# One pipeline for a ternary feed-forward network, with part of its preparation taken in the attention before it

## The reference, cut to what matters

```python
def _layernorm(x):            # what stands ahead of every sublayer
    return (x - mean(x)) / sqrt(var(x) + 1e-5)
def rmsnorm(x, weight):
    return x * rsqrt(mean(x * x) + 1e-5) * weight
def activation_quant(x):      # per row (token)
    scale = 127.0 / clip(max(abs(x)), 1e-05)
    return clip(round(x * scale), -128, 127) / scale
def weight_quant(w):          # one scale for the whole matrix; values -1, 0, 1
    scale = 1.0 / clip(mean(abs(w)), 1e-05)
    return clip(round(w * scale), -1, 1) / scale
def bitlinear(x, w):
    return einsum('bsh,oh->bso', activation_quant(x), weight_quant(w))
x_norm = rmsnorm(x, norm_weight)                     # 256 wide
gate, up = split(bitlinear(x_norm, w_gate_up))       # w_gate_up: 1408 x 256
hidden = square(relu(gate)) * up                     # 704 wide
return bitlinear(hidden, w_down)                     # w_down: 256 x 704
```

## Time and profile before

| What | Value |
|---|---|
| Median of 3 runs | 3785.6 us (3783.56 to 3797.69) |
| Profiled execution | 3776.57 us, span 3774.7 us |
| PE busy | 2875.6 us (76% of the span) |
| DVE busy | 2273.3 us (60%) |
| ACT busy | 1493.7 us (40%) |
| POOL busy | 885.2 us (23%) |

### The profile page before, as it was taken

One profiled execution on the slowest core, in us unless ns is written; L12 is line 12 of the kernel. 1 busy time (PEld: TensorE's weight loads), 2 busy tenths in 40 slices (PEclk: granted clock), 3 DMA queues, 4 the chain that ended last, 5 costly groups with the idle time before them and its releaser, 6 DMA issues. The chain is left out here.

```text
span 3774.7 us, 60424 instructions
## 1 busy us (share of the span) xinstructions
PE 2875.6 (76%) x19922; PEld 1822.1 (48%) x19922; DVE 2273.3 (60%) x5171; ACT 1493.7 (40%) x3091; POOL 885.2 (23%) x1241
## 2 busy tenths in 40 slices
PE   5388885465899993399716599899979839999993
PEld 4233334222555552233303377444547638888782
DVE  7699983676677775633467788788869730000003
ACT  5277771254222225399614355222235302121110
POOL 3111110376233336211100033000023261111110
PEclk7599995798999995599857799999989859999996
DMA  8766633499222224478100153000034321111204
GB/s 262 176 118 118 121 90 134 159 367 359 88 82 80 80 75 170 114 134 118 26 24 0 45 168 104 2 1 1 1 96 141 102 83 55 46 59 48 84 27 134
DMA packets 261309, 386.20 MB, mean 102 GB/s; under 512 B 56321, under 2 KB 188654, under 8 KB 260768
## 3 DMA queue, kind: packets, MB, share of 16 engines
q1 hardware_dynamic: 234192, 312.76, 31.1%
q0 software_dynamic: 25152, 68.22, 5.2%
q10 hardware_dynamic: 1680, 1.57, 0.2%
HBM read 227.75 MB, written 160.24 MB: 103 GB/s over the span
## 5 line engine op out<-in xcount | busy, mean ns | idle before, releaser
L3022 POOL DMA_INDIRECT rows_out<-e_out,e_tr_dest x224 | 234.7, 1048 | 872.0 <-DVE e_out L3652 521.2
L1188 ACT ACTIVATE a_pt<-a_psS 128x512 f32<-128x512 f32 x512 | 277.5, 595 | 152.1 <-PE a_psS L1086 147.7
L3652 DVE COPY e_out<-e_psD 128x512 f32<-128x512 f32 x40 | 27.7, 692 | 491.8 <-PE e_psD L3620 491.7
L1210 DVE TENSOR_REDUCE a_mx_sb<-a_psM 128x4 f32<-128x1024 f32 x256 | 292.9, 1215 | 17.2 <-PE a_psM L1069 16.0
L3420 PE MATMUL e_psG<-e_wgu,e_yT 128*128 x576 | 275.1, 600 | 27.0 <-ACT e_yT L3448 24.4
L1100 PE MATMUL a_psV<-a_pt,a_vt 128*18 128x256 f32 x4096 | 291.4, 386 | 1.3 <-issue 0.8
L3620 PE MATMUL e_psD<-e_w,e_hT 128*128 128x256 f32 x1280 | 289.7, 386 | 0.0
L3609 PE MATMUL e_psH<-e_yT,e_w 128*128 128x256 f32 x1280 | 284.4, 381 | 1.6 <-issue 0.8
L3552 ACT ACTIVATE e_hT<-e_psH 128x512 f32<-128x512 f32 x160 | 95.5, 597 | 451.8 <-PE e_psH L3609 451.8
L3620 PEld LDWEIGHTS e_psD<-e_w,e_hT 128*128 128x128 f32 x1280 | 245.8, 195 | 32.8
L3609 PEld LDWEIGHTS e_psH<-e_yT,e_w 128*128 128x128 f32 x1280 | 244.5, 191 | 35.0 <-issue 2.1
(11 more groups left out here) (420 smaller groups left out, 5997.7 us busy)
## 6 DMA issues: line engine op xcount, KB each, us to landing
kbd<-e_bgu SPq DMA_DIRECT2D x64, 512.0 KB, 4.5
cr_kbd<-kbd SPq DMA_DIRECT2D x64, 512.0 KB, 3.4
rows_in<-zeros POOLq DMA_DIRECT2D x36, 522.0 KB, 6.5
e_xin<-rows_in SPq DMA_DIRECT2D x144, 128.0 KB
vbd<-e_bd SPq DMA_DIRECT2D x64, 272.0 KB, 4.2
cr_vbd<-vbd SPq DMA_DIRECT2D x64, 272.0 KB, 2.7
cq_rows<-rows_out SPq DMA_DIRECT2D x32, 512.0 KB, 5.8
e_w<-in_L_ffn_w_dram SPq DMA_DIRECT2D x16, 1024.0 KB, 7.6
```

The lines of the kernel that those rows point to most:

```text
L1188: act.activation(pt[:, probs(t, h), b, :, :], psS[:, unit(t, h, b) % S_BANKS, :].rearrange("p (k c) -> p k c", k=KC), ACT.Exp, scale=scale ...
L1210: dve.tensor_reduce(mx[:, t % 2, :, h, :], psM[:, k % 2, :, :].rearrange("p b (f c) -> p b f c", f=2), AX_X, ALU.max).then_inc(ring_read, 1)
L3022: pool.indirect_dma_start(out=self.rows_out[0:limit, :], out_offset=bass.IndirectOffsetOnAxis(ap=self.dest[:, t:t + 1], axis=0), in_=rows, ...
```

## The change

Two things are done.

First, `phase_norms`, `phase_bit_weights`, `phase_bit_inputs` and `phase_bit_ffn` are replaced for layer 1. A new object, `BitPrelude`, puts their loads, the row statistics, the roots and the sums over the weights into the second attention: SP issues three loads at its tile 20, DVE takes the statistics of tile t - 6 behind its division of tile t and the sums of the two weight matrices at tiles 26 and 28, and POOL computes the two roots of four tiles at a time at every fourth tile, the last two groups behind the loop.

Second, all that is left is one block, `phase_bit`, whose steps are written out without hardware loops. POOL now centres and weights the inputs (two instructions per tile), cuts the down weights, and scales and rounds the 704 hidden values of each tile (two instructions). DVE keeps the row maxima and the quantisation of the inputs, spread over four steps for a group of four tiles, the product with up, the row maximum, the small operations and the residual. The residual of tile s - 3, the product of tile s and part of the inputs of a later group stand in one step of DVE; PE runs gate and up for tile s + 1, the transposes for s - 1 and the down projection for s - 2 in one step. ACT copies the turned weights, in batches of up to four blocks.

```diff
 # phase_attend, POOL
                     if t >= 4:
                         add_tile(t - 4)
+                    if prelude is not None and t >= 11 and t % 4 == 3:
+                        prelude.root(pool, (t - 11) // 4)
                 for t in range(TILES - 4, TILES):
                     add_tile(t)
+                if prelude is not None:
+                    prelude.root(pool, 6)
+                    prelude.root(pool, 7)
 # phase_attend, SP
+                    if t == 20 and prelude is not None:
+                        prelude.load(sp)
 # phase_attend, DVE
                         divide(t, psN[:, 0, :], psN[:, 1, :], scaled)
+                        if prelude is not None and t >= prelude.LAG:
+                            dve.wait_ge(added, t - prelude.LAG + 1)
+                            prelude.survey(dve, t - prelude.LAG)
+                        if prelude is not None and t in (26, 28):
+                            prelude.sum_weights(dve, (t - 26) // 2)
+                    if prelude is not None:
+                        for t in range(TILES - prelude.LAG, TILES):
+                            dve.wait_ge(added, t + 1)
+                            prelude.survey(dve, t)
+class BitPrelude:
...
+    def survey(self, dve, t):
...
+        dve.bn_stats(self.stats[:, t % 2, :], self.core.xs[:, t, :]).then_inc(self.surveyed, 1)
+        dve.wait_ge(self.surveyed, t + 1)
+        dve.bn_aggr(self.core.mv[:, t, :], self.stats[:, t % 2, :]).then_inc(self.averaged, 1)
+    def sum_weights(self, dve, m):
...
+        dve.tensor_reduce(self.part[:, m:m + 1], w[:, :, :].rearrange("p o i -> p (o i)"), AX_X, ALU.add, apply_absolute_value=True).then_inc(self.summed, 1)
+    def root(self, pool, g):
...
+        pool.wait_ge(self.averaged, (g + 1) * self.G)
...      # a Chain of 7 instructions on 4 columns, two of them ALU.pow
+def phase_bit(core, prelude, gate):
...
+                def centre(g, j):
+                    t = g * G + j
+                    if g >= 2:
+                        pool.wait_ge(rounded, g - 1)
+                    pool.tensor_scalar(z[:, g % 2, j, :], core.xs[:, t, :], core.mv[:, t, 0:1], col(prelude.rr, t), ALU.subtract, ALU.mult).then_inc(centred, 1)
+                    pool.wait_ge(centred, t + 1)
+                    pool.tensor_tensor(z[:, g % 2, j, :], z[:, g % 2, j, :], prelude.wb[:, :], ALU.mult).then_inc(z_ready, 1)
...
+                for s in range(FIRST, TILES):
+                    if s == FIRST + G:
+                        cut_down()
+                    g, j = group_at(s, 10)
+                    if g is not None:
+                        centre(g, j)
+                    t = s
+                    if ok(t):
...
+                        pool.wait_ge(scaled, t + 1)
+                        pool.tensor_scalar(flat, flat, col(scale, t), ROUND_MAGIC, ALU.mult, ALU.add).then_inc(h_scaled, 1)
+                        pool.wait_ge(h_scaled, t + 1)
+                        if t >= 2:
+                            pool.wait_ge(q_turned, t - 1)
+                        pool.tensor_scalar(q[:, t % 2, :], flat, ROUND_MAGIC, None, ALU.subtract).then_inc(quantised, 1)
...      # PE
+                for s in range(-2, TILES + 2):
...
+                    if g is not None and j == 0:
+                        turn_inputs(g)
+                    if ok(s + 1):
+                        gate_up(s + 1)
...
+                    if ok(s - 1):
+                        turn_rows(s - 1)
+                    if ok(s - 2):
+                        down(s - 2)
...      # DVE
+                for s in range(-6, TILES + 3):
+                    if ok(s - 3):
+                        residual(s - 3)
+                    t = s
+                    if ok(t):
...
+                        dve.tensor_tensor(flat, psG[:, 2:4, 0:HALF], flat, ALU.mult).then_inc(u_read, 1)
...
+                        dve.tensor_reduce(col(hm, t), flat.rearrange("p a c -> p (a c)"), AX_X, ALU.max, apply_absolute_value=True).then_inc(maxed, 1)
+                    g, piece = group_at(s, 6)
+                    if g is not None and piece != 2:
+                        inputs(g, piece)   # 0: row maxima; 1: six small ones; 3: round 1024 values
+                    if ok(t):
...
+                        c.link(dve.tensor_scalar(col(sm, t), col(hm, t), col(sgd, t), 1e-5 / 127.0, ALU.mult, ALU.max))
+                        c.link(dve.reciprocal(col(rs, t), col(sm, t)))
...
+                        dve.tensor_scalar(col(scale, t), col(rs, t), col(sg3, t), None, ALU.mult).then_inc(scaled, 1)
+                        dve.tensor_scalar(col(out, t), col(sm, t), mu[:, 1:2], gate, ALU.mult, ALU.mult).then_inc(out_ready, 1)
+                    if g is not None and piece == 2:
+                        inputs(g, piece)   # four scalings of 256 values
```

More of the change, by code:

```diff
@@ L1860, in _ @@
             @block.scalar
             def _(act):
[L1862 to L1887, removed]
+                def copy_weights(i):
+                    kind, lo, hi = W_BATCHES[i]
+                    src = bank_of[i % 2][:, 0:(hi - lo) * KC * P].rearrange("p (o k c) -> p o k c", k=KC, c=P)
+                    act.wait_ge(w_turned, i + 1)
+                    if kind == "gu":
+                        for k in range(KC):
+                            ins = act.activation(guT[:, k, lo * P:hi * P].rearrange("p (o c) -> p o c", c=P), src[:, :, k, :], ACT.Copy)
+                        ins.then_inc(w_copied, 1)
+                        return
+                    whole = min(hi, F1 // P)
+                    act.activation(downT[:, lo:whole, :].rearrange("p o (k c) -> p o k c", c=P), src[:, 0:whole - lo, :, :], ACT.Copy).then_inc(w_copied, 1)
+                    if whole < hi:
+                        rows = F1 - whole * P
+                        act.activation(downT[0:rows, whole, :].rearrange("p (k c) -> p k c", c=P), src[0:rows, whole - lo, :, :], ACT.Copy).then_inc(w_copied, 1)
@@ new lines, in _ @@
+                for s in range(-2, TILES + 1):
+                    if s == -2:
+                        for i in range(3):
+                            copy_weights(i)
+                    g, j = group_at(s, 2)
+                    if g is not None and j == 0:
+                        copy_inputs(g)
+                    if ok(s + 1):
+                        relu(s + 1)
+                        square(s + 1)
+                    if s == -1:
+                        for i in range(3, len(W_BATCHES)):
+                            copy_weights(i)
+                    if ok(s - 1):
+                        copy_rows(s - 1)
@@ L1889, in _ @@
             @block.vector
             def _(dve):
+                c = Chain(dve, mu_step)
                 dve.wait_ge(total, 1)
[L1892 to L1899, removed]
@@ new lines, in _, with inputs @@
+                dve.tensor_scalar(tg[:, :, :], w[:, :, :], -1.0, None, ALU.max).then_inc(gu_cut, 1)
+                def inputs(g, piece):
+                    v, rows = g % 2, slice(g * G, (g + 1) * G)
+                    per = 7
+                    if piece == 0:
+                        dve.wait_ge(z_ready, (g + 1) * G)
+                        dve.tensor_reduce(am[:, v, :], z[:, v, :, :], AX_X, ALU.max, apply_absolute_value=True).then_inc(am_step, 1)
+                        dve.wait_ge(am_step, g * per + 1)
+                    if piece == 1:
+                        c = Chain(dve, am_step, g, per, base=1)
+                        c.link(dve.tensor_scalar(am[:, v, :], am[:, v, :], 1e-5, 1.0 / 127.0, ALU.max, ALU.mult))
+                        c.link(dve.reciprocal(s1[:, v, :], am[:, v, :]))
+                        c.link(dve.tensor_scalar(sg[:, v, :], am[:, v, :], mu[:, 0:1], None, ALU.mult))
+                        c.link(dve.tensor_tensor(sg3[:, rows], sg[:, v, :], sg[:, v, :], ALU.mult))
+                        c.link(dve.tensor_tensor(sg3[:, rows], sg3[:, rows], sg[:, v, :], ALU.mult))
+                        c.link(dve.tensor_scalar(sgd[:, rows], sg3[:, rows], 1.0 / 127.0, None, ALU.mult))
+                    if piece == 2:
+                        for j in range(G):
+                            dve.tensor_scalar(za[:, v, j, :], z[:, v, j, :], s1[:, v, j:j + 1], ROUND_MAGIC, ALU.mult, ALU.add).then_inc(z_scaled, 1)
+                    if piece == 3:
+                        dve.wait_ge(z_scaled, (g + 1) * G)
+                        if g >= 2:
+                            dve.wait_ge(i_turned, g - 1)
+                        dve.tensor_scalar(q8[:, v, :, :], za[:, v, :, :], ROUND_MAGIC, None, ALU.subtract).then_inc(rounded, 1)
```

409 lines of the change are left out of this document (201 added, 208 removed).

## The result

The changed kernel takes 3704.2 us, the median of 3 runs (3704.15 to 3704.81), where the kernel before takes 3785.6: a ratio of 0.9784 with a 95% interval of 0.9768 to 0.9799. In a later comparison on one chip it was 0.9793 (0.9775 to 0.9810). The forecast was 3698 us, in a range from 3677 to 3728.

The account below looks back on a forecast made before the run. DVE was taken to bound a tile. 31 + 26 x 4.85 + 5 x 4.2 + 3 + 7.7 = 188.8 us replace 277.7; less 1 in the attention, 88 us off the median 3785.6 gives 3698 us, range 3677 to 3728.

Parts of the forecast that it names:

- The attention, its end, and the prelude: Second attention: the added prelude costs 1 us (bounds 0 and 8); the network's block begins 9.5 us after its end.
- rival D: Second attention: POOL's roots delay its layout of values and PE waits, 24 us, total 3722 us; chance 0.07.
- POOL's rate: POOL's wide one-input instructions run at its copy's rate: 0.42 us for 256 values, 0.81 for 704, 1.43 for 1408.
- Up to the first product: Block start to first product: 17.4 us without collisions, 22 with them, so 31 us behind the attention's end.
- the collision: Before the first product: DVE's cuts and input pieces are held by POOL's instructions, adding 4.5 us.
- A tile: Loop: DVE sets the pace, 4.85 us a tile with inputs (bounds 4.4 and 5.6).
- the prediction's own sign of that: Loop: PE waiting for the rounded hidden values at each tile while DVE idles would show that POOL bounds.
- Rival A: Loop: POOL's wide instructions near 1.6 us, or PE mostly at the lower clock; 5.6 us a tile, 3729 us; chance 0.20.
- Being held: Loop: DVE waits for POOL's instructions, mainly at the input scalings, adding 0.44 us a tile.
- The last tiles and PE: Last five tiles, without inputs: 4.2 us each, between 3.9 and 4.5, at a granted clock of 0.84.
- the ring: Loop: PE's work between two products plus DVE's residual, product and hand-overs; 3.9 us at the upper clock, 5.8 at the lower.
- Drain: From the last product to the end of the last residual: 7.7 us.

Follow-up runs that it names:

- late_prelude: The changed kernel with the prelude's loads, statistics, weight sums and roots in a block of their own behind the attention; 0.9843 of the kernel before.
- both_forms: The changed kernel with POOL's rounding of hidden values and its centring of inputs both written as multiply-adds; 0.9724 of the kernel before.
- balanced: The changed kernel with POOL's rounding and centring as multiply-adds, down weights cut on DVE, inputs scaled and rounded on POOL; 3688.3 us, 0.9710 of the kernel before.
- q_form: The changed kernel with only POOL's rounding of the hidden values written as a multiply-add; 0.9759 of the kernel before.

## Why the prediction was right, and where it was not

The time fell inside the range and 6 us from the forecast. The direction and most of the size rest on the part that held: 20 us of statistics, 30 of weights and 66 of inputs, in which PE hardly worked, now lie beside other work. By the steps of the prediction:

- *The attention, its end, and the prelude.* Right in what the prelude costs. The block starts 9.2 us behind the last addition (9.5 predicted), and rival D did not come (late_prelude). The sign that the attention ends within 1 us of 1868.5 failed: it ended at 1873.6. Of these 5.1 us 2.3 were there at its first copy, before any of the prelude, and 2.8 came within the copies, where late_prelude, without the prelude in its attention, has 3.5.
- *POOL's rate.* The step that failed: "I take the copy's, since it has one input too." Of the forms that this block uses, the copy's rate holds for multiply-add alone. The rounding cost 1.97 us instead of 0.81, the centring 1.22 instead of 0.42, the three cuts 10.2 instead of 4.3. The upper bound of 1.96 ns a value was too low as well: the rounding needs 2.5, and subtract-multiply more. The number of inputs was the wrong thing to compare by. The 0.87 ns a value was not what its own rows give (0.2 us and 0.301 for 128 values make 0.79), which changes little beside this.
- *Up to the first product.* 34.3 us instead of 21.5, the price of that step: 5.9 us in the cuts, 8 x 0.8 = 6.4 in the centring. The 4.5 us for the collision were near in size and on the wrong engine: the path goes through POOL, which DVE held for 1.5 + 2.4 = 3.9 us, while DVE's own held instructions (4.8 and 3.0 us) ended long before it had to wait for POOL.
- *A tile.* The pace was nearly right, 4.96 against 4.85 us, for a wrong reason. DVE was named as the bound, with 4.41 us of its own and 0.44 of being held. In fact POOL was, with 4.77 us and hand-overs, and the prediction's own sign of that was there: PE waits for the rounding, and DVE is busy for 85% of the time, not over 90%. DVE's work was less, 4.2 us with what it was held (99 of 116 us at 4.96), and 4.1 in both_forms (94% of 4.39). Neighbouring DVE rows overlap by some 0.08 us, so a sum of their durations is too long: in both_forms' stretch of 109 us they sum to 112 us where DVE is busy for 102. Two errors of opposite sign met, and that the pace came out is luck. Rival A's condition, wide POOL instructions near 1.6 us or more, came true as well, without its 5.6 us a tile.
- *Being held.* Right as a mechanism and about right in size: in the loop 24 scalings at 0.59 us instead of 0.35 and five small instructions on 4 columns at 0.82 instead of 0.23 make some 0.37 us a tile, an estimate, where 0.44 was taken. The Trainium skill, "SBUF — State Buffer", section Who interferes with whom, divides DVE's instructions in this way: copies, casts and multiply-adds can enter a mode that uses both ports and then exclude a GpSimd instruction, two SBUF inputs contend with one that reads SBUF, and reductions and other instructions with at most one SBUF input do not. The measured 3.1 to 4.2 us of the held ones against 0.42 of the others agree; a multiply-add on one column was not held (0.155 us). The prediction took the exclusion to last for the whole instruction; for products of two SBUF tensors the measured one ended 0.7 and 1.0 us before POOL's.
- *The last tiles and PE.* 3.82 us against 4.2. After the inputs the clock rose to 0.94, nearer to the ring's 3.9 us at the upper level. That sum was too high itself: balanced went at 3.47 us in its last six tiles.
- *Drain.* 10.8 us instead of 7.7. The rounding is 1.2 of it (1.2 less in q_form). The trace shows two terms that the sum lacked: the down projection and residual of the tile before stand behind the last transposes (2070.5 to 2072.6), of which ACT's 1.0 us, which was counted, covers a part; and the last down projection takes 1.55 us instead of 0.93, at a granted clock of 0.50.
- *The level.* The forecast took 88 us off the median. The traces give 72 us, 12.4 us less in the block and 4 in the attention than predicted, but the medians differ by 81, since the profiled execution of before was 9 us under its median. So part of the closeness is luck: by the traces the sum promised 16 us too much.

## What to carry to other kernels

Before work moves to an engine, look for a row of the same operation on it, not of the same number of inputs: on POOL the way in which one and the same arithmetic is written made a factor of 2.5. When two engines are near each other in load, a fix of one cost shows little until the next is fixed too: 0.20 and 0.17 us a tile alone, 0.57 together. And a forecast of the pace says little about its cause; ask the busy shares which engine it is.

## What the hardware showed that was not expected

- POOL, 704 fp32 values: multiply-add and min-max 0.77 us, with two column operands 0.92, cast 0.77, product of two tensors 1.67, one operation alone (add, multiply, subtract, max) 1.97 to 1.99, other pairs 2.56 to 2.58. A multiply or an add alone is dearer than the two in one instruction, and max alone dearer than min and max.
- A DVE multiply-add on 2 or 3 columns is held until POOL's instruction of 4.94 us ends (4.07 and 4.04 us), one on a single column is not (0.155), nor a reciprocal of 4 (0.178). A product of two SBUF tensors is held even on one column, but about 1 us less long (3.07).
- It holds the other way too: DVE's cuts of 2816 values made a POOL centring of 1.22 us last 3.63.
